# Edge counting by pairs of target groups in a graph network kernel, with its loop bounds and a bias add moved into mixing

## The reference

```
xn = layernorm(x)
x = x + gnn0(xn, src, dst) + mix0(xn)
x = x + experts0(layernorm(x))
xn = layernorm(x)
x = x + gat1(xn, src, dst) + mix1(xn)
x = x + experts1(layernorm(x))

mix0:  q, k, v = split(xn @ Wqkv);  q, k = elu(q) + 1, elu(k) + 1
       kv = sum over nodes of k^T v per head;  z = 1 / (q . sum k + 1e-6)
       out = (q @ kv) * z @ Wout + bout
mix1:  the same with relu, clip(q . sum k, 100), a temperature, Wproj and bproj
gnn0:  three times: normalise over nodes, then
       agg[dst] += x[src] / sqrt(out_deg[src]) over the 40000 edges, / sqrt(in_deg[dst]);  relu(agg @ W + b)
```

## Time and profile before

| what | us |
|---|---|
| median of 3 runs (2611.17 to 2612.36) | 2611.21 |
| the profiled execution | 2606.02 |
| its span, first to last instruction | 2604.2 |
| PE busy | 2239.5 (86%) |
| DVE busy | 992.9 (38%) |
| ACT busy | 514.3 (20%) |
| POOL busy | 284.8 (11%) |
| L727 PE MATMUL x416, busy | 140.1 |
| L700 DVE TENSOR_SCALAR x416, busy | 118.5 |
| first mixing, key and value part | 43 to 123.4 |
| first mixing, rest | 123.4 to 225 |
| edge counting | 225 to 435.9 |
| second mixing | 1282.5 to 1460 |

### The profile page before, as it was taken

The page is one execution under the profiler, slowest core; times in us unless marked ns, Lnnn a source line. Parts: engine busy times, 40 slices in busy tenths (PEclk is TensorE's granted clock), DMA queues, the critical chain, the costliest instruction groups (busy, mean ns, idle before and its releaser), DMA issues. The chain is left out here.

```text
span 2604.2 us, 27822 instructions
## 1 busy us (share of the span) xinstructions
PE 2239.5 (86%) x7328; PEld 1261.2 (48%) x7329; DVE 992.9 (38%) x2694; ACT 514.3 (20%) x900; POOL 284.8 (11%) x299
## 2 busy tenths in 40 slices
PE   5977777999996998887399889989989988799996
PEld 3533333444444445444254348864468844435553
DVE  6854555320204532221214355522255403624443
ACT  1111112111110302222110034301144212201111
POOL 0200000000000015444011000000000010003332
PEclk9999999999998999999799989989999999889998
DMA  3002000000000426666300100020000011247775
GB/s 113 1 0 106 1 0 1 17 0 16 0 1 0 129 69 157 160 161 127 120 0 0 56 0 1 1 89 1 0 1 1 1 37 49 73 144 227 227 233 129
DMA packets 77158, 159.33 MB, mean 61 GB/s; under 512 B 9027, under 2 KB 20334, under 8 KB 77010
## 3 DMA queue, kind: packets, MB, share of 16 engines
q1 hardware_dynamic: 59410, 115.62, 13.0%
q0 software_dynamic: 17664, 42.64, 8.0%
HBM read 122.06 MB, written 38.74 MB: 62 GB/s over the span
## 5 line engine op out<-in xcount | busy, mean ns | idle before, releaser
L1773 PE MATMUL bank<-arena 125*125 125x257 f32 x1600 | 355.8, 383 | 4.7 <-DVE arena L1692 4.7
L1773 PEld LDWEIGHTS bank<-arena 125*125 125x125 f32 x1600 | 302.2, 189 | 60.4 <-DVE arena L1692 6.3
L2011 PE MATMUL bank<-arena 128*128 x832 | 251.3, 452 | 25.2 <-issue 14.7
L881 PE MATMUL bank<-arena 125*128 125x500 f32 (+1 forms) x720 | 252.6, 513 | 2.3 <-ACT arena L906 2.3
L2011 PEld LDWEIGHTS bank<-arena 128*128 128x128 f32 x832 | 157.2, 195 | 140.7 <-issue 80.8
L1588 PE MATMUL bank<-arena 128*125 128x512 f32 x480 | 211.0, 600 | 8.8 <-DMA arena<-in_L_gnn_W 8.8
L443 PE MATMUL bank<-arena 128*125 128x512 f32 x480 | 214.1, 596 | 2.1 <-PEq L277 1.1
L2029 PE MATMUL bank<-arena 128*128 x360 | 176.2, 619 | 32.8 <-ACT arena L2057 22.3
L881 PEld LDWEIGHTS bank<-arena 125*128 125x128 f32 x720 | 135.8, 189 | 120.5 <-issue 110.6
L727 PE MATMUL bank<-arena 125*125 x416 | 140.1, 455 | 58.0 <-DVE arena L700 36.3
L2103 DVE TENSOR_TENSOR arena<-bank,arena 128x384 f32<-128x384 f32 (+1 forms) x104 | 51.6, 497 | 304.2 <-PE bank L2011 270.5
(11 more groups left out here) (322 smaller groups left out, 2188.6 us busy)
## 6 DMA issues: line engine op xcount, KB each, us to landing
arena<-in_L_ffn_expert_w SPq DMA_DIRECT2D x16, 1536.0 KB
arena<-in_L_ffn_re_w SPq DMA_DIRECT2D x32, 512.0 KB
arena<-in_L_ffn_expert_w SPq DMA_DIRECT2D x16, 768.0 KB
arena<-in_L_mix_Wqkv SPq DMA_DIRECT2D x6, 1024.0 KB, 8.2
arena<-in_L_ffn_expert_b SPq DMA_DIRECT2D x16, 384.0 KB
token_rows<-arena SPq DMA_DIRECT2D x2, 2500.0 KB
token_sums<-arena SPq DMA_DIRECT2D x20, 250.0 KB
arena<-in_L_gnn_W SPq DMA_DIRECT2D x1, 4096.0 KB, 13.0
```

The lines of the kernel that those rows point to most:

```text
L881: last = pe.matmul(st.bank[4 + n % 4][:, 0:cn], h[:, s, f * P:(f + 1) * P], st.counts[:, s, c0:c0 + cn], start=(s == 0), stop=(s == NT - 1))
L1773: return pe.matmul(st.bank[n % OUTS][0:TS, 0:ONCOL], prob[:, u % 2, s, j * TS:(j + 1) * TS], st.slots[:, head + 1, s, :], start=(s == 0), ...
L2011: last = pe.matmul(st.bank[UP[b][h]][:, 0:WP], xt[b][:, k, :], rt.ring[:, bass.ds(r, 1), k * W + h * WP:k * W + (h + 1) * WP].rearrange("p ...
```

## The change

Edge counting: each loop goes from the first bound in steps of two groups. The eight slots are used in fixed order, four for the first group of a step and four for the second, and each group has its own wait. A step may go one group past the last bound; `key` and `low_marks` are longer by one group, filled with -1 and 0, so that the group past the end counts nothing, and a group of another window has no key in this one. The bounds of the first 20 windows are loaded into registers in the first mixing, two windows a tile, on both engines; those of the last 5 stay where they were.

Mixing: the bias is added tile by tile on GpSimd, after each key sum. VectorE waits for all ten adds at the fourth query tile, and there it adds the result before it opens the product. ScalarE takes the exponential of the second query tile after it has copied m. The first block's mixing and the second's both have the first two of these; the third is in the first alone.

```
+EARLY_BOUNDS = 20
@@ set-up, VectorE
-            dve.tensor_copy(st.key, st.bank[1][0:EC, 0:NCH])
+            dve.tensor_copy(st.key[:, 0:NCH], st.bank[1][0:EC, 0:NCH])
+            dve.memset(st.key[:, NCH:], -1.0)
+            dve.memset(st.low_marks[:, NCH:, :], 0.0)
@@ mixing, GpSimd
-            pool.wait_ge(b_loaded, 16)
-            pool.tensor_tensor(st.res3, st.res3, bcast_mid(brow, NT), ALU.add).then_inc(res_biased, 1)
+                if t == 0:
+                    pool.wait_ge(b_loaded, 16)
+                pool.tensor_tensor(st.res3[:, t, :], st.res3[:, t, :], brow, ALU.add).then_inc(res_biased, 1)
@@ mixing, TensorE, in the loop over tiles
                 product(2 * t)
                 product(2 * t + 1)
+                if not relu:
+                    st.counts_bounds += [load_bounds(pe, st, w) for w in range(t * EARLY_BOUNDS // NT, (t + 1) * EARLY_BOUNDS // NT)]
                 if t >= 1:
                     kv_pair(t - 1)
@@ mixing, ScalarE
             if not relu:
                 exp(NT)
-                exp(NT + 1)
             for p in range(PAIRS):
                 act.wait_ge(m_made, p + 1)
                 act.copy(m[:, p, :], st.bank[TURN + p % 2]).then_inc(m_placed, 1)
+            if not relu:
+                exp(NT + 1)
@@ mixing, VectorE
                 open_product(2 * t, t)
                 if not relu:
+                    st.marks_bounds += [load_bounds(dve, st, w) for w in range(t * EARLY_BOUNDS // NT, (t + 1) * EARLY_BOUNDS // NT)]
...
-                open_product(n, NT + t)
                 if t == 3:
-                    dve.wait_ge(res_biased, 1)
+                    dve.wait_ge(res_biased, NT)
                 if t >= 3:
                     add_result(t - 3)
+                open_product(n, NT + t)
@@ 
-def load_bound(eng, cell, top):
-    return eng.value_load(cell, min_val=0, max_val=top)
+def load_bounds(eng, st, w):
+    NG = NCH // GROUP
+    return [eng.value_load(st.bound[w:w + 1, i:i + 1], min_val=0, max_val=NG - 1 + i) for i in range(2)]
@@ edge counting, VectorE
-                    lo = load_bound(dve, st.bound[w:w + 1, 0:1], NG - 1)
-                    hi = load_bound(dve, st.bound[w:w + 1, 1:2], NG)
-                    with dve.Fori(lo, hi, 1) as g:
+                    bounds = st.marks_bounds[w] if w < EARLY_BOUNDS else load_bounds(dve, st, w)
+                    with dve.Fori(*bounds, 2) as g:
                         n = dve.snap(made)
-                        half = dve.snap((n % 2) * GROUP)
-                        dve.wait_ge(marks_free, n + 1)
-                        for u in range(GROUP):
-                            last = dve.tensor_scalar(
-                                marks[:, bass.ds(half + u, 1), :].rearrange("p a n -> p (a n)"), st.iota16[:, 0:WIN * NT],
-                                float(w * WIN * NT), st.key[:, bass.ds(g * GROUP + u, 1)], ALU.add, ALU.is_equal)
-                        last.then_inc(marks_ready, 1)
-                        dve.reg_add(made, made, 1)
+                        keys = st.key[:, bass.ds(g * GROUP, 2 * GROUP)]
+                        for half in range(2):
+                            dve.wait_ge(marks_free, n + (half + 1))
+                            for u in range(half * GROUP, (half + 1) * GROUP):
+                                last = dve.tensor_scalar(marks[:, u, :], st.iota16[:, 0:WIN * NT], float(w * WIN * NT),
+                                                         keys[:, u:u + 1], ALU.add, ALU.is_equal)
+                            last.then_inc(marks_ready, 1)
+                        dve.reg_add(made, made, 2)
@@ edge counting, TensorE
+                    bounds = st.counts_bounds[w] if w < EARLY_BOUNDS else load_bounds(pe, st, w)
+                    with pe.Fori(*bounds, 2) as g:
                         n = pe.snap(used)
...
+                        stays = st.low_marks[:, bass.ds(g * GROUP, 2 * GROUP), :]
+                        for half in range(2):
+                            pe.wait_ge(marks_ready, n + (half + 1))
+                            for u in range(half * GROUP, (half + 1) * GROUP):
+                                last = pe.matmul(bank, stays[:, u, :], marks[:, u, :], start=False, stop=False,
+                                                 skip_group_check=True)
+                            last.then_inc(marks_free, 1)
+                        pe.reg_add(used, used, 2)
@@ memory
-        MARKS = NCH * TS // 2
+        MARKS = (NCH + GROUP) * TS // 2
-        st.key = ar.take(NCH, EC)
+        st.key = ar.take(NCH + GROUP, EC)
```

More of the change, by code:

```diff
@@ L478, in _ @@
                     turn_raw(i)
+            else:
+                st.counts_bounds = []
             for t in range(NT):
@@ L588, in _ @@
                 dve.reciprocal(st.graph_scale, st.graph_scale).then_inc(fold, 1)
+                st.marks_bounds = []
             for t in range(NT):
@@ L650, in _ @@
                 add_result(t)
-def load_bound(eng, cell, top):
-    return eng.value_load(cell, min_val=0, max_val=top)
+def load_bounds(eng, st, w):
+    NG = NCH // GROUP
+    return [eng.value_load(st.bound[w:w + 1, i:i + 1], min_val=0, max_val=NG - 1 + i) for i in range(2)]
 def stage_adjacency(nc, st, ar, first_weights):
-    NG = NCH // GROUP
     FIFTH = NW // 5
@@ L718, in _ @@
                     pe.matmul(bank, zeros[:, 0:TS], zeros, start=True, stop=False, skip_group_check=True)
-                    lo = load_bound(pe, st.bound[w:w + 1, 0:1], NG - 1)
-                    hi = load_bound(pe, st.bound[w:w + 1, 1:2], NG)
-                    with pe.Fori(lo, hi, 1) as g:
+                    bounds = st.counts_bounds[w] if w < EARLY_BOUNDS else load_bounds(pe, st, w)
+                    with pe.Fori(*bounds, 2) as g:
                         n = pe.snap(used)
[L723 to L730, removed]
+                        stays = st.low_marks[:, bass.ds(g * GROUP, 2 * GROUP), :]
[6 more added lines that the diff above has]
+                        pe.reg_add(used, used, 2)
                     pe.matmul(bank, zeros[:, 0:TS], zeros, start=False, stop=True,
@@ L2177, in build @@
         st.routed_zeroed = nc.alloc_semaphore(name="routed_zeroed")
-        MARKS = NCH * TS // 2
+        MARKS = (NCH + GROUP) * TS // 2
         ar = Arena(whole, st.counts16_at[0], words)
-        st.low_marks = ar.take(MARKS, EC).bitcast(BF16).rearrange("p (c n) -> p c n", c=NCH)
+        st.low_marks = ar.take(MARKS, EC).bitcast(BF16).rearrange("p (c n) -> p c n", c=NCH + GROUP)
         marks_end = ar.at
```

## The result

The changed kernel takes 2523.37 us (median of 4 runs, 2520.8 to 2525.57) against 2611.78 for the kernel before on the same chip: a ratio of 0.9666, 95% interval 0.9652 to 0.9680, or 88.4 us less. The prediction was 2554 with a range of 2533 to 2582: the right direction, and too little by a third. Even its case of everything good, 2533, is passed.

What follows compares the result with a forecast made beforehand. Each stretch has its own limit: counting a TensorE-VectorE hand-over, the key part a full TensorE. Gains 37.1 + 10.9 + 16.4 - 7.0 = 57.4 us took 2606.02 to 2549, plus 5.2 for the median: 2554, range 2533 to 2582.

Steps and rivals of the forecast that it cites:

- case of everything good: Rival: round trip 1.33 us a group, no turn, marks hold off GpSimd; gain 78.3 us, 2533; chance 0.12.
- The group at 1.40 us: Counting: time per group of four matmuls in the new loop, the middle of 1.46 and 1.33 us.
- The legs 0.39 and 0.35: Counting: hand-overs from marks to first matmul (0.39 us) and from matmuls' end to next mark (0.35); some 0.13 less each.
- The turn at 0.3 us: Counting: the change to the next window, 1.29 us before, falls to 0.3 with closing and opening matmul left.
- The model of the old loop: Counting: a hand-over between two engines; at the old pitch, legs through two buffers of 3.15 us, some 1.55 a group.
- The rival "not shortened": Counting: registers are recomputed as before, round trip not shortened; gain 13.4 instead of 37.1 us, 2578; chance 0.20.
- The loads moved into mixing: First mixing: TensorE's loads cost nothing, VectorE's hidden with nothing left, except 1.1 us of delay at tile 0.
- The bias by tiles in the key part: First mixing's key and value part: second GpSimd add holds up VectorE's marks; 7.0 us lost, including tile 0's 1.1.
- the one that gives the port to GpSimd: Rival, key and value part: GpSimd gets the port for both adds; 10.3 us lost instead of 7.0, 2557; chance 0.15.
- The rival of a lower clock: Key and value part: TensorE's pauses drop its clock to 1.2 GHz, some 77 us lost, 2631, slower than before; chance 0.03.
- m to the first result: First mixing: large bias add gone and exp behind the copies of m, 19.19 us becomes 8.34; 10.9 gained.
- The result add: Both mixings' query tiles: add moved ahead of the query product ends TensorE's waits of 10.3 and 6.1 us; 16.4 gained.

Runs made afterwards that it cites:

- the bias adds late: Changed kernel with GpSimd's bias add of each tile moved from behind the key add to behind that query tile's scaled rows: 2517.02 us, ratio 0.9642.
- the kernel with both undone: Changed kernel with one large bias add behind the key sums and the second exp ahead of the copies of m again: 2524.30 us, ratio 0.9678.

## Why the prediction was wrong

**The step that failed** is the size of the counting term, 37.1 us, where it measured 67.0. By the prediction's own figures 18.3 of it came from the faster group and 18.8 from the turn and the loads; in the old loop the loads alone are worth 28.9, and the new loop behind them brings 38.1 (180.6 to 142.5). The miss has four parts.

- *The group at 1.40 us.* "Sum 2.93, or 1.46 a group; with one register operation (some 0.13 us with its gap) less on each of the two hand-overs 2.67, or 1.33. I take the middle, 1.40." It is 2.53, or 1.26. The four matmuls came as forecast (1.05). The legs 0.39 and 0.35 shrank to 0.17 each, by 0.22 and 0.18 us and not by 0.13: the "0.39" was read at the first group of the stage. Taking the middle with the unshortened sum added only error: the prediction gives no reason for legs that stay.
- *The turn at 0.3 us.* It is nothing (5.04 us for four groups of 1.26). The closing and opening matmuls fit in the time in which TensorE waits for marks.
- *The last windows at 1.2 us.* 0.87 (5.92 - 5.05).
- *The clock.* The old loop ran at 0.92, the new at 1.00 from 220 us on. The sum was built on windows of 7.81 us, but the mean window of four was longer, since some ran at the low clock.

By numbers: 17 windows of four at 5.04 instead of 5.9 are 14.6 us, 3 of six at 7.58 instead of 8.7 3.4, the late ones (four at 5.92 instead of 7.1, one of six at 8.4 instead of 9.9) 6.2: 24.2 of the 29.9. The other 5.7 fit the old windows' excess: their 24 intervals took 6.0 us more than 7.79 and 9.43 for each, and with the loads alone gone the clock was 1.00. That this whole rest is the clock is inferred, not measured by itself.

The model of the old loop named the wrong limit. With the old matmul pitch its legs are 3.15, or 1.575 a group (the prediction wrote 1.55; with 1.575 its low end is 10.7 us and not 13.4), beside a measured 1.63. That is near enough to look right, but the rows of the group put TensorE's idle time down to issue, and the kernel with the old loop and early loads shows it: 1.24 + 0.40 = 1.64. The round trip sets the pace only in the changed loop. In the order in which it was taken apart, the gain came as loads early, 209.5 to 180.6; pairs, to 172.2; fixed slots, to 142.5. In the new loop the loads are worth less, 19.5 (162.0 to 142.5). The rival "not shortened" falls: with registers recomputed in pairs and early loads the counting still gains 37.3 us, and with fixed slots 67.

**The loads moved into mixing** were costed at 1.1 us and cost 3.06 by themselves: tile 0 1.94, and later tiles 1.1, most of it in the last, which I had as covered. TensorE's are hidden as said: with VectorE's out of tile 0 its first kv_pair is on time although its own loads stay.

**The bias by tiles in the key part**: 7.0 predicted for loads and adds, 6.63 measured, with the shares shifted: adds alone 4.94, loads alone 3.06, and the two overlap. So the 7.0 came out partly by luck. VectorE needs 7.95 us a tile, beside the forecast's 7.83 (half of a 1.27 us add hidden would have given 7.77). 32 marks take 5.31 us with no GpSimd add beside them, 5.94 with one, 6.83 with two. The key add, which lies 0.84 us beside them, holds them 0.63, and the second add of 1.09 us holds them 0.89. Of the rivals the one that gives the port to GpSimd is nearly true for marks; it missed for the time, in part since the second add is shorter than the 1.27 us of the key add, and in part since the first tiles still went at TensorE's 7.76 to 7.87 us.

The Trainium skill (SBUF — State Buffer, SBUF: two separate sides) has an exclusive lock on the port pair that GpSimd shares with some of VectorE's operations: the one that starts first holds it for its whole instruction, and the other stands. The trace comes near it, 0.2 us short both times: 0.63 of 0.84 us and 0.89 of 1.09.

**After the last kv_pair** 2.15 us were lost that the sum did not have. TensorE, late at the key sums and with a pause of 3.35 us ahead, ran part of the sums and of the next product at the lower clock (0.50 from 131.75 to 135.10 us):

```profile
129.86 1.16 PE L456 MATMUL bank<-arena 125*128 125x128 f32 x8 [3.35 <-DVE arena L581]
131.21 1.56 PE L498 MATMUL bank<-arena 125*125 125x512 f32 x2 [0.19 <-POOL arena L408]
132.56 4.90 PE L448 MATMUL bank<-arena 128*125 128x512 f32 x8
```

The same eight matmuls take 3.60 us at the upper level. With the bias adds late, where the pause is 0.74 us and the clock stays up, the stretch is 1.7 us shorter. The rival of a lower clock fell for the key part (1.00 over its 73 us) and was true for these few us behind it.

**m to the first result**: 10.84 for 10.9, but not for the reason given alone. The two edits together are worth 15.95 - 8.35 = 7.6 us. The other 3.2 were already gone in the kernel with both undone. 1.3 of them lie ahead of the second half of m, where the large add and the small VectorE operation behind it are shorter (9.25 and 4.98 us for 11.00 and 5.83); 1.9 lie behind it, where the kernel before ran its query product at a lower clock (0.59 from 137.40 to 147.75, 0.79 in the same stretch of the other kernel). The product in the kernel before, and with both undone:

```profile
142.81 5.11 PE L443 MATMUL bank<-arena 128*125 128x512 f32 x8
```
```profile
144.93 3.60 PE L446 MATMUL bank<-arena 128*125 128x512 f32 x8
```

TensorE had stood idle for 6.96 us ahead of the copies of m in the first and for 5.66 in the second. That the edits belong together was right; that the add itself had cost most was not. **The result add**: 10.9 + 7.75 for 10.3 + 6.1. The view of waits counts only the wait itself; the tiles of the second mixing show 8.41 to 7.30, 7 x 1.11.

## What to carry to other kernels

Before a model of a loop is used to price a change, it must give the loop as it is, and the waits that it names must be those that the rows name: here the legs summed to nearly the measured period, but the rows put TensorE's wait down to its own issue and not to the marks. Between two engines that pass buffers the first half of a gain may be in finer hand-overs over the same slots, and an engine's pace is the start-to-start time of an unbroken row of its operations, not the length of a burst with its tail. When two edits cut the same chain, each undone alone shows little: undo both before either is called harmless.

## What the hardware showed that was not expected

- The two loads of a window on each engine cost 1.28 us in the single-step loop and 0.8 to 0.9 in the paired one. On VectorE in mixing four loads a tile left it idle for 1.25 us, six for 2.49: 0.62 us a load once the lead is used up, the price that the prediction had read from the old loop.
- A second computed address on mark and matmul cost 0.25 us a group of four (1.51 against 1.26), though marks themselves came no slower (0.26 us from start to start either way).
- The large GpSimd add took 11.00 us in the one profiled execution of the kernel before and 9.25 in each of the three other kernels that have it, the same instruction on the same shapes; the small VectorE operation behind it 5.83 and 4.09 to 4.99. The cause was not looked for; what these kernels share is a layout shifted by the longer arrays of marks and keys.
- TensorE's granted clock in the counting (245 to 335 us) went from 0.92 to 1.00 when the pauses at the loads went, with nothing else changed in the loop. The loads alone do not bring the dips, though: the paired loop with its loads in the counting was at 1.00 from 220 to 370 us.
